# A vision tower on one core: image 0's embedding between position matmuls, one set of norm statistics, stacks per head, images written out

## Chip, cores and metric

One core of one Trainium2 chip runs the kernel. The metric is the device time of one execution in microseconds; the median of the runs counts.

## The reference

Eight images of 3x512x512 become 1024 tokens each of width 256. In float32:

```python
h = patches @ Wp + bp + (relu(xy @ W1 + b1) @ W2 + b2)          # tokens and positions
a = layernorm(h)                                                 # (x - m) / sqrt(var + 1e-5)
n = layernorm(a) * gamma + beta                                  # the attention norms again
q, k, v = split(n @ W_qkv.T); gate = sigmoid(a @ W_gate.T + b_gate)
h = h + a + (attention(q, k, v) * gate) @ W_final.T + b_final    # 8 heads of 32
x = layernorm(h); H = gelu(x @ F1 + c1); p = softmax(H @ Wg + bg)
h = h + p[e] * (H @ Wd[e] + bd[e])                               # e = argmax p, of 8 experts
```

The first norm is taken of h, the second of its result a; both have no weights of their own but gamma and beta.

## The kernel before, in words

Five engines run programs of their own, tied by semaphores. `over_images` (L214) runs `image` for image 0, then three times through a hardware loop whose body is two images (1 to 6), then for image 7. After that come routing (from L1061) and the expert stage over 72 slots of 128 tokens (from L720).

**Opening.** SP loads posin, posw1, posw2 and posbias (L251), 20 constants (L253 to L259), then image 0's tiles into two buffers `xt` (L262). TensorE makes the position table: four K=3 matmuls into banks 0 to 3 (L426), ScalarE's Relu (L758), and for each of eight tiles two matmuls by posw2 (L433) and one K=2 matmul that adds the biases (L434); ScalarE copies to `posb` (L761). Then `front_start` (L604) embeds eight tiles of image 0 (six K chunks each, L444), VectorE adds `posb` (`embedded`, L917), takes statistics of h (`stats`, L899, L903), GpSimd makes rstd (`root`, L339, L342: add eps, then power -0.5), VectorE writes a (L909), does the same on a, and writes n. TensorE transposes n and a (`turn`, L456), projects q and k of the first four heads (`project`, L465), ScalarE and VectorE split them into high and low parts `qk` (L785, L936). fp32 matmuls stand in the trace as two records each.

**Stacks.** `load_stack` (L275) copies, for each of four heads, three high/low pairings of q and of k into `stq` and `stk` (partitions 0 to 31, 32 to 63, 64 to 95), 24 copies of 128 KB, all counted by one semaphore per head group. `score` (L477) waits for all 24 at the group's first step. While they go, TensorE does `values` (L505) and `gates` (L511).

**Steps.** An image has 64 steps, eight token blocks for four heads, twice. Step k: two score matmuls, VectorE's maximum (L1029), ScalarE's Exp (L842), and later `weigh` (L491). Tables (L233 to L244) say at which step TensorE puts in other work: projections of the second group (steps 0 to 7), the next image's embedding (8 to 31), gates, turns and projections of the next image (35 on). At step 32 VectorE does the next image's `norm_1`, `stats_2` and `norm_2` (L1020 to L1026), TensorE the router of the image before (`norm_turn`, `router`), GpSimd both roots, then h + a + b_final (L351, L353) after n is ready. Image 0 has no router in its middle. At an image's start VectorE closes the image before (`gated`, `added` L964, `stats_3`).

## Time and profile before

| | |
|---|---|
| median of 3 runs (1948.21 to 1954.45) | 1952.97 us |
| profiled execution, its own time | 1954.93 us |
| its span | 1952.8 us |
| TensorE, VectorE, ScalarE, GpSimd busy | 89%, 59%, 52%, 16% |
| mean granted TensorE clock | 0.954 |

The span goes from the first to the last instruction; the execution's own time has 2.1 us more. A share of busy time is a mean over stages with different limits.

### The profile page before, as it was taken

The page shows a single profiled execution, that of the slowest core. Times are in us where ns is not written, and L with a number is a line of the kernel's source. Part 1 is how long each engine was busy: PE and PEld are TensorE (multiplying, and loading weights), DVE is VectorE, ACT ScalarE, POOL GpSimd, SP SyncE. Part 2 cuts the span into 40 slices and gives each one's busy share as a digit, 9 for nine tenths or more (in the row PEclk, how much of TensorE's full clock was granted, in tenths as well). Part 3 has the DMA queues.
Part 4 walks back from the last instruction along what each step waited for, and adds up shares of the span by engine and source line. Part 5 has one row for each costly group of instructions (what it writes and reads, how often), then busy time and mean ns, then how long its engine had stood idle before and what let it go on. Part 6 is the DMA issues. An engine that isn't in the chain of part 4 may idle for free.

```text
span 1952.8 us, 32763 instructions
## 1 busy us (share of the span) xinstructions
PE 1728.6 (89%) x11396; PEld 1180.4 (60%) x11396; DVE 1151.3 (59%) x1899; ACT 1012.5 (52%) x1692; POOL 309.7 (16%) x239
## 2 busy tenths in 40 slices
PE   8587899999998999999899999999797724899998
PEld 4354456646655574566467555745363614899998
DVE  0347767467655856675667468566726278344443
ACT  1144756675574657566746656585666350222222
POOL 0200100200010020002000200200000061455554
PEclk9898999999999999999999999999899867899999
DMA  3133042313413140424033222413040160566663
GB/s 112 34 98 98 1 103 77 125 30 99 112 65 82 63 133 28 103 69 133 18 103 92 93 65 73 129 39 87 17 135 1 60 220 1 200 205 199 208 204 132
DMA packets 68112, 187.59 MB, mean 96 GB/s; under 512 B 14173, under 2 KB 14829, under 8 KB 67824
## 3 DMA queue, kind: packets, MB, share of 16 engines
q1 hardware_dynamic: 51952, 121.48, 22.0%
q0 software_dynamic: 16000, 63.98, 10.0%
q8 instruction: 101, 1.65, 0.4%
q14 instruction: 59, 0.48, 0.1%
HBM read 84.72 MB, written 51.38 MB: 70 GB/s over the span
## 4 chain that ended last, share of the span: by engine, by line
PE 72%; DVE 14%; issue 8%; ACT 4%; DMA 1%; SPq 1%; POOL 0%; DVEq 0%; ACTq 0%; POOLq 0%
PE ps L477 12%; PE ps L738 11%; PE ps L491 10%; PE ps L444 8%; DVE nmax L1029 6%; PE ps L548 3%; PE ps L465 3%; PE ps L726 3%; PE ps L549 3%; PE ps L550 3%; PE ps L527 3%; PE ps L505 3%; PE ps L576 3%; ACT pr L842 2%; DVE oh L1084 2%
## 5 line engine op out<-in xcount | busy, mean ns | idle before, releaser
L1029 DVE TENSOR_REDUCE nmax<-ps 128x1 f32<-128x1024 f32 x512 | 625.2, 1222 | 315.1 <-PE ps L477 305.5
L842 ACT ACTIVATE pr<-ps,nmax 128x1024 f32<-128x1024 f32 x512 | 569.9, 1113 | 295.8 <-DVE nmax L1029 290.6
L477 PE MATMUL ps<-stk,stq 96*128 96x512 f32 x1024 | 407.3, 480 | 80.2 <-ACT pr L842 54.1
L477 PEld LDWEIGHTS ps<-stk,stq 96*128 96x128 f32 x1024 | 168.5, 193 | 282.7 <-ACT pr L842 169.0
L491 PE MATMUL ps<-pr,vs 128*32 128x256 f32 x4096 | 275.9, 391 | 16.7 <-DVE vs L948 16.6
L738 PE MATMUL ps<-wd,hg 128*128 x1728 | 225.5, 287 | 0.0
L339 POOL TENSOR_SCALAR vare<-mv 128x8 f32<-128x8 f32 x24 | 5.7, 238 | 1349.8 <-DVE mv L903 1349.8
L738 PEld LDWEIGHTS ps<-wd,hg 128*128 128x128 f32 x1728 | 212.7, 192 | 0.0
L491 PEld LDWEIGHTS ps<-pr,vs 128*32 128x32 f32 x4096 | 109.8, 110 | 166.6 <-issue 75.5
L879 ACT ACTIVATE hg<-ps 128x512 fp32r<-128x512 f32 x144 | 78.5, 596 | 249.6 <-PE ps L726 249.6
L444 PE MATMUL ps<-wp,xt 128*128 128x256 f32 x768 | 198.3, 385 | 1.6 <-DMA xt<-x_in 0.8
L444 PEld LDWEIGHTS ps<-wp,xt 128*128 128x128 f32 x768 | 146.2, 192 | 32.6 <-DMA xt<-x_in 3.1
L811 ACT ACTIVATE ht<-ps,bf 128x512 f32<-128x512 f32 x128 | 88.3, 690 | 115.5 <-PE ps L550 115.5
L465 PE MATMUL ps<-nt,wqk 128*128 128x512 f32 x256 | 132.3, 602 | 3.9 <-DVE qk L936 3.2
L1148 DVE TENSOR_TENSOR hg<-ps,hg 128x512 fp32r<-128x512 f32 x144 | 93.0, 686 | 48.9 <-ACT hg L879 48.8
L548 PE MATMUL ps<-nt_high,wf 128*128 128x512 f32 x256 | 110.7, 432 | 1.7 <-DVE nt_low L985 1.4
L549 PE MATMUL ps<-nt_low,wf 128*128 128x512 f32 x256 | 101.9, 398 | 0.0
L550 PE MATMUL ps<-nt_high,wf 128*128 128x512 f32 x256 | 101.3, 396 | 0.0
L1155 DVE SCALAR_TENSOR_TENSOR rows<-ps,slot_prob,rows 128x256 f32<-128x256 f32 x72 | 34.8, 484 | 111.1 <-PE ps L740 111.1
L842 ACT ACTIVATION_READ_ACCUMULATOR pr<-ps,nmax 128x1 f32 x512 | 99.5, 194 | 0.0
L404 POOL DMA_INDIRECT out<-rows,slot_to x72 | 72.3, 1004 | 123.2 <-DVE rows L1155 116.3
L726 PE MATMUL ps<-ident,rows 128*128 128x128 f32 x576 | 76.4, 277 | 6.6 <-DMA rows<-token_rows,slot_from 6.6
(123 smaller groups left out, 1944.2 us busy)
## 6 DMA issues: line engine op xcount, KB each, us to landing
token_rows<-staged SPq DMA_DIRECT2D x128, 256.0 KB, 2.0
xt<-x_in SPq DMA_DIRECT2D x64, 384.0 KB, 3.1
stq<-qk SPq DMA_DIRECT2D x192, 128.0 KB, 2.4
stk<-qk SPq DMA_DIRECT2D x192, 128.0 KB, 2.5
token_rows<-hres POOLq DMA_DIRECT2D x8, 1024.0 KB, 5.2
wd_raw<-w_down SPq DMA_DIRECT2D x16, 512.0 KB, 4.0
rows<-token_rows,slot_from POOLq DMA_INDIRECT x72, 4.7
out<-rows,slot_to POOLq DMA_INDIRECT x72, 2.6
```

What stands on the lines that cost most here:

```text
L444: last = mm(spare(t)[:, 0:D], xt[:, t % 2, k, :], wp[:, k, :], start=(k == 0), stop=(k == KC - 1))
L465: last = mm(spare(j), wqk[:, c, w * D + g * P:w * D + (g + 1) * P], nt[:, c, hf * HALF:(hf + 1) * HALF], start=(c == 0), stop=(c == DC - 1))
L477: last = mm(ps[:, 2 * (k % SR) + j, :], stq[:, hh, i * P:(i + 1) * P], stk[:, hh, j * 512:(j + 1) * 512], start=True, stop=True)
L491: last = mm(ps[32 * hh:32 * hh + 32, O_BANK + j // 2, (j % 2) * D:(j % 2 + 1) * D], vs[:, gi % 2, hh, :], pr[:, (4 * gi + hh) % PR, j * D: ...
L548: mm(spare(bank), w_high, nt_high[:, c, half], start=(c == 0), stop=False)
L549: mm(spare(bank), w_high, nt_low[:, c, half], start=False, stop=False)
L550: last = mm(spare(bank), w_low, nt_high[:, c, half], start=False, stop=(c == DC - 1))
L726: last = nc.tensor.transpose(ps[:, 2 * (s % 2) + c, q * P:(q + 1) * P], rows[:, s % RING, (4 * c + q) * P:(4 * c + q + 1) * P], ident[:])
L738: mm(o, hg[:, s % 2, h_part, k, :], wd[:, w_part, bass.ds(e, 1), k, :], start=(k == 0 and h_part == w_part), stop=False)
L842: actv(pr[:, k % PR, :], ps[:, 2 * (k % SR):2 * (k % SR) + 2, :].rearrange("p a n -> p (a n)"), ACT.Exp, bias=nmax[:, k % 16:k % 16 + 1], ...
L1029: V.reduce_max(nmax[:, k % 16:k % 16 + 1], ps[:, 2 * (k % SR):2 * (k % SR) + 2, :].rearrange("p a n -> p (a n)"), AX_X, negate=True).then_ ...
L1148: V.tensor_tensor(hg[:, s % 2, 1, 4 * c:4 * c + 4, :].rearrange("p k n -> p (k n)"), ps[:, 2 * (s % 2) + c, :], high_part.bitcast(F32), AL ...
```

## The change

- TensorE does the K=3 matmuls (now in banks 4 to 7), then embeds tiles 0 to 3 of image 0 into banks 0 and 1, then goes on with two position tiles and one embedding tile in turn. Six of image 0's tiles are loaded into free room of `pr`, without waits; ScalarE's queue loads wp, posw2 and posbias (on all partitions). The bias matmul is gone: VectorE adds the bias as it writes `posb`. Seven constants are `early`, twelve are waited for later, and w_ffn1 comes into `hres[:, 1]`.
- a and n are both written from h: rstd of n is (var * (1 + eps) + eps^2)^-0.5; GpSimd makes both with one power on 128x16. n is written first.
- `stq` and `stk` are one tensor; one copy of 256 KB carries a pairing of q and k: 12 a set, each head with its own semaphore, and `score` waits in the first four steps of a group for its head.
- `over_images` writes out all eight images with constant semaphore values.

The diff, without semaphore names and with unchanged lines left out:

```diff
-        stq = tensor(sa, "stq", [96, 4, TOKENS], F32R)
-        stk = tensor(sa, "stk", [96, 4, TOKENS], F32R)
+        st = tensor(sa, "st", [96, 2, 4, TOKENS], F32R)
+        stq, stk = st[:, 0], st[:, 1]
...
-        x_in, stacked = both("x_in"), both("stack")
+        x_in = both("x_in")
+        stacked = [[S[f"stack{g}{hh}"] for hh in range(4)] for g in range(GROUPS)]
+        qk_parts = qk[:].rearrange("p w a t -> p (w a) t")
+        STACK = ((0, 3, 2), (1, 3, 1), (0, 4, 3))
...
-        posbias = at[0:2, 1, 0:D]
-        wf1_in = a[:].rearrange("p (c t) d -> p c (t d)", c=DC)
-        N_CONSTS = 20
+        posbias = at[:, 1, 0:2 * D].rearrange("p (a d) -> p a d", a=2)
+        x_first = pr[:, 2:7].rearrange("p a n -> p (a n)")[:, 0:(TILES - 2) * KC * P].rearrange(
+            "p (t k n) -> p t k n", t=TILES - 2, k=KC)
+        wf1_in = hres[:, 1].rearrange("p (c t) d -> p c (t d)", c=DC)
+        N_CONSTS, N_EARLY = 12, 7
...
-            body(0, 0, False, True)
-            with eng.Fori(0, (IMAGES - 2) // 2) as j:
-                body(j * 2 + 1, 1, True, True)
-                body(j * 2 + 2, 0, True, True)
-            body(IMAGES - 1, (IMAGES - 1) % 2, True, False)
+            for b in range(IMAGES):
+                body(b, b % 2, b > 0, b < IMAGES - 1)
...
-            for dst, src in ((posin, pos_in), (posw1, pos_w1), (posw2, pos_w2), (posbias, pos_bias)):
-                sp.dma_start(dst, src).then_inc(S["pos_in"], 16)
-            for dst, src in ((wp[:], w_patch), (ident[:], identity), (vecs[:, 0, :], ln_gamma),
-                             (vecs[:, 1, :], ln_beta), (vecs[:, 2, :], b_gate), (wqk[:], w_qk), (wv[:], w_v),
-                             (wg[:], w_gate), (wfin[:], w_final), (bfin[:], b_final), (wf1_in, w_ffn1),
-                             (bf1[:], b_ffn1), (wr[:], w_router), (pick[:], pick_in), (up[:], upper),
-                             (rnk[:], rank), (brt[:], b_router), (sst[:], slot_start), (tid[:], token_id),
-                             (col[:], column)):
+            for dst, src in ((posin, pos_in), (posw1, pos_w1)):
+                sp.dma_start(dst, src).then_inc(S["pos_in0"], 16)
+            for t in range(2):
+                sp.dma_start(xt[:, t], x[0, t]).then_inc(x_in[t], 16)
+            for t in range(2, TILES):
+                sp.dma_start(x_first[:, t - 2], x[0, t]).then_inc(S[f"x_first{t // 2 - 1}"], 16)
+            for dst, src in ((vecs[:, 0, :], ln_gamma), (vecs[:, 1, :], ln_beta), (vecs[:, 2, :], b_gate),
+                             (ident[:], identity), (wqk[:], w_qk), (wv[:], w_v), (wg[:], w_gate)):
+                sp.dma_start(dst, src).then_inc(S["early"], 16)
+            for dst, src in ((bfin[:], b_final), (wf1_in, w_ffn1), (wfin[:], w_final), (bf1[:], b_ffn1),
+                             (wr[:], w_router), (pick[:], pick_in), (up[:], upper), (rnk[:], rank), (brt[:], b_router),
+                             (sst[:], slot_start), (tid[:], token_id), (col[:], column)):
...
-                    for r in range(3):
-                        if rear and hh * 3 + r >= 8:
-                            store_hidden(b - 1, hh * 3 + r - 8)
-                        src = slice(32 * hh, 32 * hh + 32)
-                        dst = slice(32 * r, 32 * r + 32)
-                        sp.dma_start(stq[dst, hh, :].bitcast(F32), qk[src, 0, r % 2, :].bitcast(F32)
-                                     ).then_inc(stacked[g], 16)
-                        sp.dma_start(stk[dst, hh, :].bitcast(F32), qk[src, 1, r // 2, :].bitcast(F32)
-                                     ).then_inc(stacked[g], 16)
...
-            load_tile(0, 0)
-            load_tile(0, 1)
-            load_rest(0)
+                    if rear and hh == 3:
+                        for u in range(4):
+                            store_hidden(b - 1, u)
+                    src = slice(32 * hh, 32 * hh + 32)
+                    for r, (first, end, step) in enumerate(STACK):
+                        sp.dma_start(st[32 * r:32 * r + 32, :, hh, :].bitcast(F32),
+                                     qk_parts[src, first:end:step, :].bitcast(F32)).then_inc(stacked[g][hh], 16)
...
-            def root(ln, b):
...
-                hold(pool, f"var{ln}", b + 1)
-                nc.gpsimd.tensor_scalar(vare[:, ln - 1], mv[:, ln - 1, :, 1], EPS, None, ALU.add
-                                        ).then_inc(S[f"eps{ln}"], 1)
-                wait(pool, f"eps{ln}", b + 1)
-                nc.gpsimd.tensor_tensor(rstd[:, ln - 1], vare[:, ln - 1], half_neg[:], ALU.pow
-                                        ).then_inc(S[f"rstd{ln}"], 1)
+            def root_1(b):
...
+                hold(pool, "var1", b + 1)
+                nc.gpsimd.tensor_scalar(vare[:, 0], mv[:, 0, :, 1], EPS, None, ALU.add).then_inc(S["eps1"], 1)
+                nc.gpsimd.tensor_scalar(vare[:, 1], mv[:, 0, :, 1], 1.0 + EPS, EPS * EPS, ALU.mult, ALU.add
+                                        ).then_inc(S["eps1"], 1)
+                wait(pool, "eps1", 2 * b + 2)
+                nc.gpsimd.tensor_tensor(rstd[:, 0:2], vare[:, 0:2], half_neg[:], ALU.pow).then_inc(S["rstd1"], 1)
...
+            def root_3(b):
+                hold(pool, "var3", b + 1)
+                nc.gpsimd.tensor_scalar(vare[:, 2], mv[:, 2, :, 1], EPS, None, ALU.add).then_inc(S["eps3"], 1)
+                wait(pool, "eps3", b + 1)
+                nc.gpsimd.tensor_tensor(rstd[:, 2], vare[:, 2], half_neg[:, 0], ALU.pow).then_inc(S["rstd3"], 1)
...
-                root(1, b)
-                root(2, b)
+                root_1(b)
...
-                hold(pool, "n_ready", b + 1)
+                hold(pool, "a_ready", b + 1)
...
+            pool.wait_ge(S["consts"], 16 * N_CONSTS)
...
-                    root(3, b - 1)
+                    root_3(b - 1)
...
-            root(3, IMAGES - 1)
+            root_3(IMAGES - 1)
...
-            pe.wait_ge(S["pos_in"], 16 * 4)
+            def position(t):
+                o = ps[:, 4 + t // 2, (t % 2) * D:(t % 2 + 1) * D]
+                for c in range(DC):
+                    last = mm(o, posr[:, c, t * P:(t + 1) * P], posw2[:, c, :], start=(c == 0), stop=(c == DC - 1),
+                              skip_group_check=True)
+                last.then_inc(S["pos_mm2"], 1)
...
+            def first_embed(t):
+                if t < 2:
+                    wait(pe, x_in[t], 16)
+                elif t % 2 == 0:
+                    wait(pe, f"x_first{t // 2 - 1}", 32)
+                source = xt[:, t] if t < 2 else x_first[:, t - 2]
+                for k in range(KC):
+                    last = mm(ps[:, t // 2, (t % 2) * D:(t % 2 + 1) * D], source[:, k, :], wp[:, k, :],
+                              start=(k == 0), stop=(k == KC - 1), skip_group_check=True)
+                last.then_inc(S["emb_mm"], 1)
...
+            pe.wait_ge(S["pos_in0"], 16 * 2)
...
-                    mm(ps[:, 2 * c + hf, :], posw1[:, c * P:(c + 1) * P], posin[:, hf * HALF:(hf + 1) * HALF],
+                    mm(ps[:, 4 + 2 * c + hf, :], posw1[:, c * P:(c + 1) * P], posin[:, hf * HALF:(hf + 1) * HALF],
...
+            pe.wait_ge(S["wp_in"], 16)
+            for t in range(4):
+                first_embed(t)
+            pe.wait_ge(S["pos_in1"], 16 * 2)
...
-            pe.wait_ge(S["setup"], 1)
-            for t in range(TILES):
-                o = ps[:, 4 + t // 2, (t % 2) * D:(t % 2 + 1) * D]
-                for c in range(DC):
-                    mm(o, posr[:, c, t * P:(t + 1) * P], posw2[:, c, :], start=(c == 0), stop=False, skip_group_check=True)
-                mm(o, ones[0:2, :].bitcast(F32), posbias, start=False, stop=True, skip_group_check=True).then_inc(S["pos_mm2"], 1)
-            pe.wait_ge(S["pos_done"], 4)
+            for t in range(4):
+                position(2 * t)
+                position(2 * t + 1)
+                first_embed(t + 4)
...
-                    wait(pe, x_in[t % 2], b * 64 + 16 * (t // 2 + 1))
+                    wait(pe, x_in[t % 2], b * 64 - 32 + 16 * (t // 2))
...
-                wait(pe, "n_ready", b + 1)
+                wait(pe, ("n_ready", "a_ready")[w // 2], b + 1)
...
-                if k % G_STEPS == 0:
-                    wait(pe, stacked[g], (b * 24 + 24) * 16)
+                if k % G_STEPS < 4:
+                    wait(pe, stacked[g][hh], (b + 1) * 3 * 16)
...
-                for t in range(TILES):
-                    for part in range(3):
-                        embed(b, t, part)
-                wait(pe, "emb_h", b * TILES + TILES)
+                wait(pe, "pos_done", 4)
...
+            pe.wait_ge(S["early"], 16 * N_EARLY)
+            front_start(0)
...
-            front_start(0)
...
+            nc.scalar.dma_start(wp[:], w_patch).then_inc(S["wp_in"], 16)
+            nc.scalar.dma_start(posw2, pos_w2).then_inc(S["pos_in1"], 16)
+            nc.scalar.dma_start(posbias, pos_bias[None, :, :].broadcast_to([P, 2, D])).then_inc(S["pos_in1"], 16)
...
-                actv(posr[:, j // 2, (j % 2) * HALF:(j % 2 + 1) * HALF], ps[:, j, :], ACT.Relu).then_inc(S["pos_relu"], 1)
-            for j in range(4):
-                act.wait_ge(S["pos_mm2"], 2 * j + 2)
-                actv(posb[:, 2 * j:2 * j + 2, :].rearrange("p t d -> p (t d)"), ps[:, 4 + j, :], ACT.Identity
-                     ).then_inc(S["pos_done"], 1)
...
-            act.wait_ge(S["consts"], 16 * N_CONSTS)
-            actv(wf1[:, 0], wf1_in, ACT.Identity).then_inc(S["wf1_high"], 1)
+                actv(posr[:, j // 2, (j % 2) * HALF:(j % 2 + 1) * HALF], ps[:, 4 + j, :], ACT.Relu).then_inc(S["pos_relu"], 1)
+            act.wait_ge(S["early"], 16 * N_EARLY)
...
-                    if g == 0:
-                        wait(act, stacked[1], b * 24 * 16)
-                    else:
-                        wait(act, stacked[0], (b * 24 + 24) * 16)
+                    for hh in range(4):
+                        if g == 0:
+                            wait(act, stacked[1][hh], b * 3 * 16)
+                        else:
+                            wait(act, stacked[0][hh], (b + 1) * 3 * 16)
...
+            act.wait_ge(S["consts"], 16 * N_CONSTS)
+            actv(wf1[:, 0], wf1_in, ACT.Identity).then_inc(S["wf1_high"], 1)
...
-            dve.wait_ge(S["consts"], 16 * N_CONSTS)
+            dve.wait_ge(S["pos_in1"], 16 * 2)
+            V.tensor_tensor(posbias[:, 0], posbias[:, 0], posbias[:, 1], ALU.add).then_inc(S["pos_sum"], 1)
+            dve.wait_ge(S["early"], 16 * N_EARLY)
...
-            dve.wait_ge(S["setup"], 2)
-            dve.wait_ge(S["wf1_high"], 1)
-            V.tensor_tensor(wf1[:, 1], wf1_in, wf1[:, 0].bitcast(F32), ALU.subtract
-                            ).then_inc(S["setup"], 1)
...
+                aggregate(b, ln)
...
+            def aggregate(b, ln):
...
-                hold(dve, f"rstd{ln}", b + 1)
+                hold(dve, "rstd1", b + 1)
...
-                    last = V.tensor_scalar(dst[:, t, :], src[:, t, :], mv[:, ln - 1, t, 0:1],
-                                           rstd[:, ln - 1, t:t + 1], ALU.subtract, ALU.mult)
+                    last = V.tensor_scalar(dst[:, t, :], src[:, t, :], mv[:, 0, t, 0:1], rstd[:, ln - 1, t:t + 1],
+                                           ALU.subtract, ALU.mult)
...
-                wait(dve, "emb_mm", b * TILES + t + 1)
+                wait(dve, "emb_mm", b * TILES + (t + 1 if b else t // 2 * 2 + 2))
...
-                V.tensor_tensor(hres[:, par, t, :], spare(t)[:, 0:D], posb[:, t, :], ALU.add).then_inc(S["emb_h"], 1)
+                source = spare(t)[:, 0:D] if b else ps[:, t // 2, (t % 2) * D:(t % 2 + 1) * D]
+                V.tensor_tensor(hres[:, par, t, :], source, posb[:, t, :], ALU.add).then_inc(S["emb_h"], 1)
...
-                normalise(a, hres[:, par], b, 1, "a_ready")
...
-            def stats_2(b):
-                wait(dve, "a_ready", b + 1)
-                stats(a, b, 2)
...
-            def norm_2(b, before):
...
+            def norm_2(b, par, before):
...
-                normalise(n, a, b, 2, "n_ready")
+                normalise(n, hres[:, par], b, 2, "n_ready")
+                normalise(a, hres[:, par], b, 1, "a_ready")
...
+            dve.wait_ge(S["pos_sum"], 1)
+            dve.wait_ge(S["setup"], 2)
...
+                if t % 2 == 0:
+                    wait(dve, "pos_mm2", t + 2)
+                    V.tensor_tensor(posb[:, t:t + 2, :], ps[:, 4 + t // 2, :].rearrange("p (t d) -> p t d", t=2),
+                                    posbias[:, 0, None, :].broadcast_to([P, 2, D]), ALU.add).then_inc(S["pos_done"], 1)
+                    wait(dve, "pos_done", t // 2 + 1)
...
-            norm_1(0, 0)
-            stats_2(0)
-            norm_2(0, False)
+                if t >= 1:
+                    wait(dve, "emb_h", t)
+                    V.bn_stats(bst[:, 0, t - 1, :], hres[:, 0, t - 1, :])
+            wait(dve, "emb_h", TILES)
+            V.bn_stats(bst[:, 0, TILES - 1, :], hres[:, 0, TILES - 1, :]).then_inc(S["stats1"], 1)
+            aggregate(0, 1)
+            norm_2(0, 0, False)
...
+            dve.wait_ge(S["wf1_high"], 1)
+            V.tensor_tensor(wf1[:, 1], wf1_in, wf1[:, 0].bitcast(F32), ALU.subtract).then_inc(S["setup"], 1)
...
-                            stats_2(b + 1)
...
-                            norm_2(b + 1, before)
+                            norm_2(b + 1, 1 - par, before)
```

## Rows read from the trace of the kernel before

**Rows 1.** The page's fourth part: the chain that ended last, by engine.

```profile
PE 72%; DVE 14%; issue 8%; ACT 4%; DMA 1%; SPq 1%; POOL 0%; DVEq 0%; ACTq 0%; POOLq 0%
```

**Rows 2.** Windows, one image each: length, engines busy, PEclk, DMA share, GB/s.

```profile
254.97:432.31 177.34, 168.92 (x1106) 105.84 (x1105) 117.45 (x201) 113.25 (x192) 16.03 (x9) 1.00 0.30 84
...
609.58:793.72 184.14, 173.19 (x1106) 108.51 (x1105) 117.55 (x201) 113.36 (x192) 15.86 (x9) 0.97 0.29 81
793.72:972.22 178.50, 170.08 (x1105) 106.00 (x1104) 117.59 (x201) 113.98 (x193) 15.86 (x9) 0.99 0.30 84
972.22:1155.59 183.37, 173.03 (x1106) 108.47 (x1105) 117.24 (x200) 112.64 (x190) 15.86 (x9) 0.97 0.29 81
1155.59:1332.90 177.31, 168.90 (x1105) 105.82 (x1105) 117.35 (x201) 113.27 (x192) 15.86 (x9) 1.00 0.30 84
```

**Rows 3.** Chain of waits of the opening: start us, us, what.

```profile
4.40 7.21 PE ps L426 x8
...
12.28 2.07 PE ps L433 x4
14.35 1.15 PE ps L434 x2
...
38.26 5.50 PE ps L444 x12
...
61.69 2.87 PE ps L444 x12
```

**Rows 4.** Timeline, opening, norms: start, us, engine, line, operation.

```profile
64.58 0.42 DVE L917 TENSOR_TENSOR hres<-ps,posb 128x256 f32<-128x256 f32 x1 [2.52 <-PE ps L444]
...
67.79 0.64 DVE L903 BATCH_NORM_AGGREGATE mv<-bst 128x2 f32<-128x6 f32 x8
68.62 0.24 POOL L339 TENSOR_SCALAR vare<-mv 128x8 f32<-128x8 f32 x1 [67.63 <-DVE mv L903]
68.95 1.67 POOL L342 TENSOR_TENSOR rstd<-vare,half_neg 128x8 f32<-128x8 f32 x1
...
81.70 1.94 PE L456 MATMUL ps<-ident,n 128*128 128x128 f32 x8 [17.16 <-DVE n L909]
```

**Rows 5.** Timeline, opening, stacks and first scores.

```profile
97.81 0.61 SPq L285 DMA_DIRECT2D stq<-qk  x1
...
115.81 1.22 PE L477 MATMUL ps<-stk,stq 96*128 96x512 f32 x2 [7.37 <-DMA stk<-qk]
...
122.15 0.73 PE L477 MATMUL ps<-stk,stq 96*128 96x512 f32 x2 [0.34 <-ACT pr L842]
```

**Rows 6.** Timeline, middle of image 0, VectorE.

```profile
179.61 2.70 DVE L899 BATCH_NORM_STATS2 bst<-hres 128x6 f32<-128x256 f32 x8
...
197.09 2.36 DVE L1029 TENSOR_REDUCE nmax<-ps 128x1 f32<-128x1024 f32 x2
```

**Rows 7.** Timeline, start of image 1: first copy, fourth score.

```profile
254.05 0.53 SPq L285 DMA_DIRECT2D stq<-qk  x1
...
278.83 0.90 PE L477 MATMUL ps<-stk,stq 96*128 96x512 f32 x2
```

**Rows 8.** Waits: VectorE for the router's partial logits.

```profile
DVE lt L992 <- PE ps L558: 77.1, 16, 17.6
```

**Rows 9.** Windows of the opening: as in rows 2.

```profile
4.40:12.20 7.80, 7.19 (x8) 2.49 (x8) 0.00 (x0) 2.36 (x4) 0.00 (x0) 1.00 1.02 369
...
108.50:115.80 7.30, 0.00 (x0) 0.00 (x0) 0.00 (x0) 0.66 (x1) 0.00 (x0) 0.79 0.91 195
```

**Rows 10.** The page's sixth part: one group of copies, us to landing.

```profile
stq<-qk SPq DMA_DIRECT2D x192, 128.0 KB, 2.4
```

**Rows 11.** Chain of waits, start of image 1 and first return of the loop.

```profile
254.97 3.65 PE ps L505 x16
...
609.58 2.69 issue
612.27 6.47 PE ps L505 x16
```

8 lines of the change are left out of this document (4 added, 4 removed).

## The prediction

> **What bounds the kernel now.** I read the chain of waits first. TensorE carries 72% of it and VectorE 14% [rows 1]; no transfer bounds the whole, so a part of the change counts only where TensorE stands still or works on something avoidable. The table by image comes next: the six images between the first and the last take 177.3 us three times, and 184.1, 178.5 and 183.4 us the other times [rows 2]. The last two-thirds of the span are thus a steady machine, with irregularities at two places. The opening is the opposite: the first score matmul of image 0 starts at 115.8 us, and before it the chain is a list of single engines, one after another [rows 3 to 5]. After that I looked at the middle of image 0, the only one that has no router of an earlier image between its two head groups [rows 6], at the start of image 1 [rows 7], and at who waits during the routers [rows 8].
>
> **Opening, tokens (front part).** Now: first matmuls at 4.40, when the last of four small loads has landed; 7.21 us for the K=3 matmuls; eight position tiles of 2.01 + 1.15 us, to 37.6; the first embedding tile 5.50 us, the later ones 2.87 us, with a 0.3 us wait for the input buffer between them, the last ending at 64.56 [rows 3]. After: only two small loads stand before the first matmul; issued 0.7 us earlier, so it starts at 3.7 and the K=3 matmuls end at 10.9. wp now comes on ScalarE's queue behind at most a table load of 1.28 us, and shares the engines with the eight image tiles. wp and the first four tiles are 2.3 MB; at the 369 GB/s of the opening [rows 9] that is 6.3 us, landed by about 10, and tiles 2 and 3 are wanted only near 19. All other early constants are 2 MB more and wanted at 50. I therefore cost the loads at nothing; were they not covered, SP's issue (0.4 us a load) would delay wp's neighbours by 2 to 3 us.
>
> What remains is TensorE's rate. The profile's granted clock is 1.00 from the start [rows 9], but the same 128x256 matmuls take half a microsecond per record until 43.8 us and a quarter afterwards [rows 3]: I go by durations, so this is the lower level (1.2 GHz), then the higher (2.4 GHz). It rose 5.5 us after TensorE had gone over to nothing but full K=128 matmuls, and not in 26 us of busy position work with K=2 matmuls among it. Image 0 goes over to full matmuls at 10.9, so one tile at 5.5 and three at 2.87 end at 25.0. Then four rounds of two position tiles (2 x 4 records of 0.24 us = 1.9; the bias matmuls, 1.15 us each, are gone, VectorE adds the bias) and one embedding tile (2.87): 19.1 us, to 44.1. VectorE's work of a round is one 128x512 addition (at most two of 0.42 [rows 4]), two of 0.42 and two statistics of 0.34 (an eighth of 2.70 [rows 6]), 2.4 us beside TensorE's 4.8: hidden. Gain here: 64.6 - 44.1 = **20.4 us**.
>
> The rule of the Trainium skill that bears on this, "TensorE: Matmul & The Clock Gate", section "What's actually happening", says that the throttled state is the default and that busy time releases it. By it the clock would be up before the embedding starts, and the sum 2.6 us lower. The trace does not agree: busy throughout and slow for 39 us.
>
> **Opening, norms.** Now 0.42 us for the last addition, 2.7 + 0.64 for the statistics, POOL's root, 2.7 for a, then all of it again for n: TensorE transposes at 81.70, 17.1 us after the embedding [rows 4]. After: five of the eight statistics run beside TensorE; two additions, three statistics, the aggregation and gaps leave 2.7 us instead of 3.9. POOL then does two cheap operations (0.24) and one pow on 128x16. The trace has pow only at 128x8: 1.67 us [rows 4]. Bounds: 1.67 (all fixed) and 3.34 (all per element). A cheap operation of the same size takes 0.24, so little is fixed: 3.2 us. Root with gaps 4.0, n 2.7, start 0.1: the transposes begin 9.5 us after the embedding. The transposes of a wait until 2.7 us after n, where now they follow the 1.94 us of n's [rows 4] at 2.05: 0.7 lost. Gain: 17.1 - 9.5 - 0.7 = **6.9 us**. POOL's two additions of 4.5 us start after a is ready and are wanted only at the end of image 0.
>
> wf1's two halves move behind the projections of image 0; ScalarE (1.9 us) and VectorE (2.3 us) are otherwise idle while TensorE does values and gates (10.7 us). Nothing.
>
> **Opening, stacks.** Now 24 copies are issued 0.64 us apart from 97.81 and the first score waits for all: 18.0 us [rows 5], although TensorE had finished values and gates after 10.7 (7.37 us wait [rows 5]). The fourth score starts 24.3 us after the first issue. The DMA engines are 0.91 busy at 195 GB/s in that stretch [rows 9], so 12 copies of twice the size can't go much faster: I take 15.5 us for the set plus 2.1 to land, 17.6 for head 3; heads 0, 1, 2 at about 6, 10, 14. The scores of heads 0 to 2 then start at 10.7, 12.4 and 14.8, and the fourth at 17.6, where head 3 binds. Gain at the fourth: **6.7 us**. Bounds: 0 and 7.4.
>
> **Middle of image 0.** VectorE's chain from 179.61 to the maximum at 197.09 [rows 6] loses one set of statistics (3.4 us) and one root (2.1), and gains 1.5 + 0.3 for the wider root: **3.7 us**. The stack for the second group is late next, but only its first heads are wanted at once: head 0 at 183, head 3 near 194, its score near 197.5. That the scores wait for stk meanwhile is a wait beside VectorE's, and doesn't count twice.
>
> **Images 1 to 7.** The saved statistics save nothing: VectorE stands still for the router's partial logits 77 us in all [rows 8]. n and a now follow each other behind keep_logits, 2.7 us more there, more than 10 us before its next maximum. At an image's start the stack is issued from 254.05, its last copy lands 18 us later, near 272, and TensorE comes to the fourth score at 278.83 [rows 7]: hidden before and after. In the second group the router covers both; the four hidden stores now stand together ahead of head 3, and end in the router too.
>
> **Images written out.** The loop comes back twice. At 609.58 TensorE issues nothing for 2.69 us, and its next matmuls take 6.47 us, where the same ones take 3.65 us in image 1 [rows 11]: 5.5 us of image 3's surplus of 6.8 over 177.3 [rows 2]. That leaves 1.3 us for some matmuls at the lower level later in the image; image 4, which no return precedes, has a surplus of 1.2 too, and image 5's 6.1 are then a return of 4.8 and 1.3. The granted clock of these three is 0.97, 0.99 and 0.97, of the others 1.00 [rows 2]. Entering and leaving the loop costs nothing visible. I take the 10.3 us of the two returns and, as the short falls came in half the images, about a third of the other 3.8: **11.5 us**. Bounds: 0 (nothing bound to the loop) and 14.1.
>
> **Sum:** 20.4 + 6.9 + 6.7 + 3.7 + 11.5 = 49.2 us. The profiled execution took 1954.9 us: 1905.7; it is 2.0 us above the median of the three runs (1952.97), so the median becomes 1903.8, **1904 us**. Image 7's end, routing and the expert stage (from 1521 us) are not touched.
>
> **Rivals.**
> - *The clock stays low.* If position work among the embedding keeps TensorE at the lower level, eight tiles of 5.5 and eight of 2.01 end at 10.9 + 60.1 = 71.0, not 44.1: 27 us dearer, **1931 us**. For: the slow 26 us of position work [rows 3]. Against: K=2 matmuls are gone, and four full tiles stand ahead. 0.09.
> - *The clock rises with any busy time*, so already in the K=3 matmuls, and the first embedding tile takes 2.87 in place of 5.50: 2.6 us less, **1901 us**. Against: 39 slow us. 0.04. This is the rule of the Trainium skill named above.
> - *Returns cost the same without a loop*, as stretches of fetching code that the loop only happens to show: no 11.5 us, **1915 us**. This is also the case in which writing out doesn't do what it should. Against: image 6, reached in straight code, has no surplus, and image 1, the first inside, has none either [rows 2]. 0.10.
> - *Slower: the paired copies.* Each copy now gathers two strided rows of qk per partition. If the set of 12 takes S us instead of 18, the fourth score of every later image is late by S - 24.8 (254.05 to 278.83 [rows 7]), seven times; image 0 loses S - 17.6 at its start and about S - 21 in its middle. It eats the 49 us at S = 29, that is 2.4 us a copy where two now take 1.28. At twice the present time, S = 36: 78 + 18 + 15 = 111 us, **2015 us**. For: no such pattern in the trace. Against: of the 2.4 us to a 128 KB copy's landing [rows 10] the bytes at 195 GB/s are 0.7, the rest has nothing to do with size, and the pieces per partition stay 4 KB long. 0.04.
> - My forecast: 0.73.
>
> **Range.** Own bounds of the likeliest: down by 2.6 (clock), 3 (pow, twice), 0.7 (stacks) and 2.6 (loop), 9 us: 1895; up by two more slow tiles (5.3), loads (2.5), stacks (3), loop (5) and VectorE's round (1): 1921. That takes in two rivals; 1931 and 2015 stay out, so 1895 to 1922. What a measurement can tell from no change is 0.3%, 6 us; every case but the last is far beyond it: faster 0.94, same 0.02, slower 0.04.
>
> **What would show it.** First score of image 0 near 82 us in place of 115.8; embedding of image 0 ended near 44 with 2.87 us tiles from the second on; one pow of about 3.2 us per image; six middle images at 177 to 179 us; no issue gap at 610 and 972. Wrong, if embedding tiles stay at 5.5 us, if TensorE waits for stacks at image starts, or if the middle images keep 180 us and more.

## Result and profile after

| | before | after |
|---|---|---|
| median of four runs | 1953.31 us (1948.21 to 1954.45) | 1896.16 us (1895.51 to 1899.28) |
| span of the profiled execution | 1952.8 us | 1896.9 us |
| mean granted TensorE clock | 0.954 | 0.964 |

The kernel is faster: ratio 0.9715, 95% interval 0.9695 to 0.9736. The forecast was 1904 us with a range of 1895 to 1922; the gain is 57.2 us by the medians and 55.9 us by the spans, against a sum of 49.2. The working below goes by the spans of one profiled execution each (that of after is the slowest of its four), which are cut at four instants: end of the opening (fourth score matmul of image 0), first values matmul of image 1, the same of image 7, end.

| stretch | before | after | gain | forecast |
|---|---|---|---|---|
| start to fourth score | 122.15 | 86.11 | 36.0 | 34.0 |
| to image 1 | 132.8 | 129.8 | 3.0 | 3.7 |
| images 1 to 6 | 1077.9 | 1062.3 | 15.6 | 11.5 |
| image 7 to the end | 619.9 | 618.7 | 1.3 | 0 |

The chain by engine, fourth part of the page after; it answers to [rows 1]:

```profile
PE 72%; DVE 13%; issue 7%; ACT 5%; DMA 2%; SPq 1%; POOL 0%; DVEq 0%; ACTq 0%; POOLq 0%
```

"DMA" rose from 1% to 2%: transfers bind in a few places more, the opening above all. Its chain shows them (start us, us, what; it answers to [rows 3 to 5]):

```profile
1.22 4.24 DMA pr<-pos_w
5.50 7.19 PE ps L449 x8
12.69 12.05 PE ps L442 x48
24.74 1.73 PE ps L431 x8
26.46 2.59 PE ps L442 x12
...
39.41 2.60 PE ps L442 x12
...
45.35 2.95 POOL rstd L342
48.32 2.67 DVE n L932 x8
...
59.56 7.15 PE ps L489 x16
...
80.93 5.14 DMA st<-qk
86.11 0.73 PE ps L501 x2
```

Read it as a ladder. The second of two small loads lands late, and TensorE starts at 5.50, 1.1 us later than before. The first four embedding tiles take 12.05 us; four at the later pace (2.59) would take 10.4, so little of this stretch was slow. Then rounds of 1.73 and 2.59 follow without a gap, to 42.0 us (before 64.56). One power, then n (a and the transposes follow in lines left out); the projections start at 59.56. The last step is a transfer: the copy for head 3 lands 5.1 us after its issue, and the fourth score waits for it.

The middle of image 0, VectorE's timeline (as [rows 6]):

```profile
144.53 2.70 DVE L919 BATCH_NORM_STATS2 bst<-hres 128x6 f32<-128x256 f32 x8
...
151.57 2.67 DVE L932 TENSOR_SCALAR n<-hres,mv,rstd 128x256 f32<-128x256 f32 x8 [3.66 <-POOL rstd L342]
...
157.93 2.34 DVE L1061 TENSOR_REDUCE nmax<-ps 128x1 f32<-128x1024 f32 x2
```

From statistics to maximum 13.4 us, before 17.5 [rows 6]: 4.1 gained. One us of that is not a loss of this stretch: a pair of projections at half speed (1.71 us instead of 0.86) stood before the fourth score in the kernel before and stands behind it now, at 89.14.

The windows by image (columns as in [rows 2]):

```profile
215.92:392.47 176.55, 168.82 (x1105) 105.71 (x1105) 113.83 (x185) 113.23 (x192) 15.55 (x8) 1.00 0.31 84
...
922.08:1101.68 179.60, 170.31 (x1105) 105.91 (x1105) 113.85 (x185) 113.30 (x192) 15.39 (x8) 0.99 0.30 83
1101.68:1278.21 176.53, 168.78 (x1106) 105.65 (x1105) 113.85 (x185) 113.20 (x192) 15.39 (x8) 1.00 0.31 84
```

Five of the six images take 176.5 us, three of which had 177.3 [rows 2]: 0.8 us that no step of the forecast contained. VectorE is 3.5 us less busy in each, the saved statistics; that is not where the 0.8 are from (experiments 1 and 5). The waits say where those went: VectorE now waits 129.8 us for the router's partial logits, before 77.1 [rows 8].

```profile
DVE lt L1012 <- PE ps L582: 129.8, 16, 17.4
```

ScalarE's timeline has the 0.8 us. Image 1 before:

```profile
374.08 0.60 ACT L798 ACTIVATE staged<-ps 128x512 f32<-128x512 f32 x1 [0.40 <-DMA token_rows<-staged]
375.34 1.28 ACT L842 ACT_TABLE_LOAD   x1 [0.66 <-DVE nmax L1029]
```

And after:

```profile
334.63 0.60 ACT L818 ACTIVATE staged<-ps 128x512 f32<-128x512 f32 x1 [0.24 <-DMA token_rows<-staged]
335.24 1.28 ACT L864 ACT_TABLE_LOAD   x1
```

The Exp needs a table that the router's Gelu displaced. Before, the load of 1.28 us itself waited for the maximum; after, it starts with the end of the last `staged` copy. In the groups of instructions, the seven loads of before (images 1 to 7) stand in one row, with 4.0 us of idle time ahead of them; in after it is 0.1:

```profile
L842 ACT ACT_TABLE_LOAD x7 | 9.0, 1283 | 4.0 <-DVE nmax L1029 4.0
```

Image 5 of after is 3.1 us longer. The chain has one transfer there at nearly twice its usual time, the twelfth of the sixteen stores of the router's hidden values (`staged`) in that image. It takes 2.0 us as a rule, and ScalarE waits for its buffer:

```profile
1038.76 3.42 DMA token_rows<-staged
```

### The profile page after: what moved, and what is told of

It is laid out like the page before. It is cut to its first block, busy times and chain, and to the rows that moved or that the text cites. A ratio compares the mean times of both kernels' runs of the same rounds, so it can differ in the third digit from the quotient of the medians.

```text
span 1896.9 us, 29956 instructions
## 1 busy us (share of the span) xinstructions
PE 1696.9 (89%) x11380; PEld 1165.0 (61%) x11380; DVE 1125.5 (59%) x1776; ACT 1009.6 (53%) x1688; POOL 306.0 (16%) x231
## 3 DMA queue, kind: packets, MB, share of 16 engines
q0 software_dynamic: 16000, 63.98, 10.4%
## 4 chain that ended last, share of the span: by engine, by line
PE 72%; DVE 13%; issue 7%; ACT 5%; DMA 2%; SPq 1%; POOL 0%; DVEq 0%; ACTq 0%; POOLq 0%
PE ps L501 12%; PE ps L760 11%; PE ps L515 11%; PE ps L468 8%; DVE nmax L1061 5%; PE ps L572 3%; PE ps L748 3%; PE ps L489 3%; PE ps L574 3%; PE ps L573 3%; ACT pr L864 3%; PE ps L551 3%; PE ps L529 3%; PE ps L600 2%; DVE oh L1116 2%
## 5 line engine op out<-in xcount | busy, mean ns | idle before, releaser
L501 PE MATMUL ps<-st 96*128 96x512 f32 x1024 | 403.8, 477 | 69.3 <-ACT pr L864 54.6
L501 PEld LDWEIGHTS ps<-st 96*128 96x128 f32 x1024 | 167.0, 192 | 272.3 <-ACT pr L864 140.9
L468 PE MATMUL ps<-wp,xt 128*128 128x256 f32 x672 | 172.8, 378 | 0.0
L468 PEld LDWEIGHTS ps<-wp,xt 128*128 128x128 f32 x672 | 126.3, 189 | 25.3 <-DVE qk L956 1.3
L346 POOL TENSOR_SCALAR vare<-mv 128x8 f32<-128x8 f32 x8 | 1.9, 239 | 718.5 <-DVE mv L926 718.5
L1012 DVE COPY lt<-ps 128x512 f32<-128x512 f32 x16 | 11.1, 692 | 129.8 <-PE ps L582 129.8
```

The source lines that it names most:

```text
L468: last = mm(spare(t)[:, 0:D], xt[:, t % 2, k, :], wp[:, k, :], start=(k == 0), stop=(k == KC - 1))
L501: last = mm(ps[:, 2 * (k % SR) + j, :], stq[:, hh, i * P:(i + 1) * P], stk[:, hh, j * 512:(j + 1) * 512], start=True, stop=True)
```

## Experiments

Every kernel was measured beside the kernel before on the same chip; those medians are 1951.3 to 1952.6 us.

**1. The loop alone, written out** in the kernel before:

```diff
-            body(0, 0, False, True)
-            with eng.Fori(0, (IMAGES - 2) // 2) as j:
-                body(j * 2 + 1, 1, True, True)
-                body(j * 2 + 2, 0, True, True)
-            body(IMAGES - 1, (IMAGES - 1) % 2, True, False)
+            for b in range(IMAGES):
+                body(b, b % 2, b > 0, b < IMAGES - 1)
```

> The kernel before, its image loop written out, nothing else. Then the six middle images take 176.5 us each (177.3, 184.1, 178.5, 183.4 before), 15 to 19 us in all, and the time is about 1936. Rival: the 0.8 us per image belongs to the stacks or the norms; then the images stay at 177.3, the gain is 14 us or less and the time 1939 or more. Second rival: it is fetching that the loop only shows; no gain, 1953.

Measured: 1937.28 us, ratio 0.9917 (0.9889 to 0.9946), 15 us less. Windows of images 1, 2 and 5:

```profile
254.15:436.43 182.28, 172.94 (x1105) 108.41 (x1105) 117.39 (x201) 113.20 (x192) 16.03 (x9) 0.97 0.29 82
436.43:613.00 176.57, 168.80 (x1105) 105.69 (x1105) 117.34 (x201) 113.23 (x192) 15.89 (x9) 1.00 0.30 84
...
966.49:1147.37 180.88, 171.60 (x1105) 106.53 (x1105) 117.24 (x201) 113.22 (x192) 15.86 (x9) 0.98 0.29 82
```

The base of 176.5 us is there with the old norms and old copies, and the table load's idle time is 0.1 us. So the 0.8 us per image belong to the loop. Laid side by side, TensorE's matmuls in image 1 of the kernel before stay within 0.3 us of those in image 2 of this one up to the table load, and are 0.6 to 1.1 us late from there on.

Images 1 and 5 are longer than the base by 10.1 us together: the twelfth hidden store takes 3.92 and 3.84 us there, and the granted clock falls to 0.97 and 0.98. So the six images gain only 8.2 us in this execution (1069.8 against 1077.9); 4.6 us more of its span's gain lie behind image 7's start, where nothing was changed, and are spread.

**2. Without the K=2 matmuls.** The kernel before, with no bias added to the position table:

```diff
-                    mm(o, posr[...], posw2[:, c, :], start=(c == 0), stop=False, ...)
-                mm(o, ones[0:2, :].bitcast(F32), posbias, start=False, stop=True, ...).then_inc(S["pos_mm2"], 1)
+                    last = mm(o, posr[...], posw2[:, c, :], start=(c == 0), stop=(c == DC - 1), ...)
+                last.then_inc(S["pos_mm2"], 1)
```

> The kernel before without the K=2 matmul that adds the biases to a position tile (the biases are left out of the result). Theory: the K=2 matmuls keep TensorE at the lower level; without them it rises some 4 us into the position tiles, their last records take 0.22 us in place of 0.50, position ends near 22 us in place of 37.6 and the first embedding tile takes 2.6 us in place of 5.5: 18 us less, 1935. Rival: only the embedding raises the rate; records stay at 0.50, position ends near 28.4, the first embedding tile still takes 5.5: 9 us less, 1944.

Measured: 1934.26 us (one run). Its chain:

```profile
12.39 9.24 PE ps L433 x32
...
22.31 2.87 PE ps L445 x12
```

The 32 position records take 9.24 us; in the kernel before they take 16 (eight times 2.01), with 9.2 of bias matmuls between them [rows 3]. The first embedding tile is fast at once.

**3. K=2 replaced by K=128.** The same work for TensorE, at full height, with another bias in the sums:

```diff
-                mm(o, ones[0:2, :].bitcast(F32), posbias, start=False, stop=True, ...)
+                mm(o, ones[:].bitcast(F32), posw2[:, 0, :], start=False, stop=True, ...)
```

> The kernel before with the K=2 bias matmul replaced by one with K=128 (ones by the first chunk of posw2 in place of the biases, so the biases in the result are others): the same number of matmuls, columns and weight loads. Theory: few rows of the array at work keep the clock low; with 128 rows it rises some 4 us into the position tiles, which end near 25 us in place of 37.6, and the first embedding tile is fast: 15 us less, 1938. Rival: the number of short matmuls and the pauses between groups keep it low, however many rows: no change, 1953.

Measured: 1942.18 us (one run). Its chain:

```profile
15.16 1.71 PE ps L433 x4
16.87 0.85 PE ps L434 x2
17.72 1.03 PE ps L433 x4
18.75 0.43 PE ps L434 x2
```

The pairs halve at 17.7 us (0.85 to 0.43, and the groups of four from 1.71 over 1.03 to 0.86), though the instructions are as many as before. What kept TensorE slow for 39 us was thus the low matmuls and what comes with them, not the number of matmuls. One thing changed together with the height: at the same lower level four records and a pair take 1.71 and 0.85 us here, where the kernel before needs 2.01 and 1.15, 0.3 us more at every change between K=128 and K=2. This experiment doesn't show that these pauses had no part in it. The K=3 matmuls have no such changes among them, though, and 7.2 us of them left the level low too. Image 1 starts 13.5 us earlier (241.49); images 1 to 6 took 1079.8 us in this execution, 1.9 more than in the kernel before.

**4. A semaphore per head, 24 copies as before:**

```diff
-                if k % G_STEPS == 0:
-                    wait(pe, stacked[g], (b * 24 + 24) * 16)
+                if k % G_STEPS < 4:
+                    wait(pe, stacked[g][hh], (b + 1) * 6 * 16)
```

> The kernel before with one semaphore per head for the same 24 copies of 128 KB. Theory: the gain of the stacks comes from the semaphores alone, since the engines set the pace of the set: first score of image 0 10.7 us after the first issue in place of 18.0, the fourth about 18 in place of 24.3; 5 to 6 us less, 1947.5. Rival: pairing q and k is needed; with 24 copies head 3 lands after 20 us or more and the gain is under 3 us. In images 1 to 7 nothing in either.

Measured: 1946.06 us, ratio 0.9971 (0.9957 to 0.9984). The first copy is issued at 97.04; the scores of heads 0 and 1 start at 107.1 and 108.4, those of heads 2 and 3, from the timeline:

```profile
111.35 0.73 PE L478 MATMUL ps<-stk,stq 96*128 96x512 f32 x2 [1.03 <-DMA stk<-qk]
...
115.35 0.74 PE L478 MATMUL ps<-stk,stq 96*128 96x512 f32 x2 [2.41 <-DMA stk<-qk]
```

The fourth comes 18.3 us after the first issue, against 24.3 before and 18.0 after (68.08 to 86.11). Nearly all of the stack term is the finer wait; pairing q and k in one copy neither helps nor hurts by more than 0.3 us.

**5. The shared statistics alone** in the kernel before (n and a both from h, one power on 128x16):

```diff
-                normalise(n, a, b, 2, "n_ready")
+                normalise(n, hres[:, par], b, 2, "n_ready")
+                normalise(a, hres[:, par], b, 1, "a_ready")
```

> The kernel before with the changed kernel's norms alone (one set of statistics, one power on 128x16, n and a both from h, n first). Theory: a gain only in image 0, where nothing covers the chain: 4.9 us in the opening (one set of statistics 3.4, one root 2.1, less 1.3 for the wider power and 0.2 for its second cheap operation, and 0.6 back because a comes last), 4.1 us in its middle, nothing in images 1 to 7, where VectorE goes on waiting for partial logits: 8 to 9 us in all, 1944. Rival: images 1 to 6 gain 0.8 us each too, since VectorE is free earlier; then 1939, and images of 176.5 us inside the loop.

Measured: 1944.08 us, ratio 0.9959 (0.9943 to 0.9974). Timeline of its opening, and the first score of the middle:

```profile
68.76 2.94 POOL L343 TENSOR_TENSOR rstd<-vare,half_neg 128x16 f32<-128x16 f32 x1
...
74.56 1.94 PE L461 MATMUL ps<-ident,n 128*128 128x128 f32 x8 [10.48 <-DVE n L914]
...
188.33 2.08 PE L482 MATMUL ps<-stk,stq 96*128 96x512 f32 x4 [12.36 <-DMA stk<-qk]
```

The power takes 2.94 us. The first score comes 5.8 us earlier (110.0 against 115.8), image 1 starts 7.8 earlier (247.17), so the middle gives 2.0. There VectorE's chain has shrunk, but the one semaphore for 24 copies now ends last and returns the rest. In images 1 to 6 nothing is won: image 1 takes 177.3 us, as before. This is the check on the saved statistics: 3.4 us less work an image, no time.

**6. Position tiles first, then the embedding,** in the kernel after:

```diff
-            for t in range(4):
-                first_embed(t)
-            pe.wait_ge(S["pos_in1"], 16 * 2)
-            pe.wait_ge(S["pos_relu"], 4)
-            for t in range(4):
-                position(2 * t)
-                position(2 * t + 1)
-                first_embed(t + 4)
+            for t in range(TILES):
+                position(t)
+            pe.wait_ge(S["wp_in"], 16)
+            for t in range(TILES):
+                first_embed(t)
```

> The changed kernel with its eight position tiles ahead of its eight embedding tiles, not between them. Theory: the order is worth next to nothing; what it replaced was slow for its K=2 matmuls and for the waits for the input. TensorE waits 0.7 us for the last Relu, the position tiles take the slow start instead of the embedding, and VectorE's additions, which now come in one row at the end, still keep up with 2.6 us a tile: image 0's embedding ends 0 to 1.5 us later, 1896 to 1898. Rival: the position tiles between the embedding hide VectorE's and the loads' work; without them the first transposes come 4 us later or more, 1900.

Measured: 1892.71 us, ratio 0.9691 (0.9674 to 0.9707), no slower than after; the forecast was 1896 to 1898. Its chain:

```profile
13.23 9.12 PE ps L431 x32
22.35 20.73 PE ps L442 x96
```

The embedding ends at 43.1 instead of 42.0, and image 1 starts at 217.23 instead of 215.92. Neither is beyond chance: in after and in kernels 9, 11 and 12, whose openings are the same code, the embedding ends at 42.0, 43.4, 42.1 and 43.0, the fourth score starts at 86.1 to 87.3, and image 1 at 215.9 to 218.5. The order that gives the change its name is worth nothing that can be told; the token term is the missing bias matmuls, the clock that rises early without them, and the loads that no longer wait for a buffer.

**7. Image 1's norms spread over image 0's steps** (statistics beside the embedding from step 8 on, two of the 16 writes of n and a in each of the steps 34 to 41):

```diff
+                    if after and not before and G_STEPS + 2 <= k < G_STEPS + 10:
...
+                        for t in (m % 4 * 2, m % 4 * 2 + 1):
+                            last = V.tensor_scalar(dst[:, t, :], hres[:, 1 - par, t, :], mv[:, 0, t, 0:1],
+                                                   rstd[:, ln - 1, t:t + 1], ALU.subtract, ALU.mult)
```

> The changed kernel with image 1's norms spread over image 0's steps (statistics tile by tile behind the embedding in steps 8 to 31, the power beside gated and two maxima, n and a two tiles a step in steps 34 to 41), images 2 to 7 as they are. Theory: in the middle of image 0 two chains run side by side, VectorE's (13.4 us from 144.5) and the copies of the second group's heads (18 us from 141.7, head 3 at 159.8). With VectorE's gone the copies bind, and the fourth score of the group, now at 161.7, comes near 159.8: only 1 to 2 us less, 1894. Rival: VectorE's chain is what sets it and the copies have room; then 9 us less, 1887.

**8. The same, with each head's copies released by that head's last score:**

```diff
-                hold(sp, "score_mm", b * STEPS + g * G_STEPS)
                 for hh in range(4):
+                    hold(sp, "score_mm", b * STEPS + g * G_STEPS - 3 + hh)
```

> The kernel a_mid with, besides, each head's copies released by that head's own last score (steps 28 to 31) in place of the last score of all heads. Theory: the set of copies starts 5.5 us earlier, head 3 lands near 154, and both chains are gone together: the fourth score of the second group near 154 in place of 161.7; 7 to 8 us less than the changed kernel, 1888. In images 1 to 7 the copies are hidden before and after. Rival: the earlier copies take the engines from the input loads or the stores of other images and cost in all eight images; then 1896 or more.

Measured: 1892.68 us (one run) for 7 and 1894.25 us, ratio 0.9702 (0.9686 to 0.9718), for 8. Timeline of the second head group's last score that waits, in 7 and then in 8:

```profile
159.60 1.22 PE L501 MATMUL ps<-st 96*128 96x512 f32 x2 [2.35 <-DMA st<-qk]
```

```profile
155.74 1.22 PE L501 MATMUL ps<-st 96*128 96x512 f32 x2 [2.22 <-DMA st<-qk]
```

With VectorE's norms out of the way the copies bind, as forecast (159.8), and releasing them earlier moves the score up by 3.9 us (forecast 154). But image 1 starts at 217.93 in 7 and at 214.93 in 8, against 215.9 to 218.5 for after's opening: of the 6 us by which kernel 8 beats after's 161.7 at that score, 1 to 3.6 are left, and the 1888 us forecast for it are missed. The norms had been moved into steps that VectorE's maximum already paces, so they came back one step at a time. The chain of 8 shows the pattern:

```profile
164.25 1.23 DVE nmax L1065
165.47 0.64 DVE a L1090 x2
166.12 1.13 DVE nmax L1065
```

**9. Idle matmuls as filler** in the last image's steps, to keep the clock up where the kernel after shows 0.95 for the image:

```diff
+                    if not after and (11 <= k < G_STEPS or k >= G_STEPS + 8):
...
+                        mm(spare(k)[:, 0:D], xt[:, 0, 0, :], wp[:, 0, :], start=True, stop=True)
```

> The changed kernel with one idle matmul (two records of 0.22 us, result unused) a step in steps 11 to 31 and 40 to 63 of the last image, which has no embedding, turns or projections of a next one. Theory: the last image takes 181 to 188 us from run to run because TensorE has pauses there and its granted clock falls (1.00 in the run with 181.4, 0.83 and 0.95 in two stretches of the changed kernel's with 187.5); VectorE and ScalarE set the pace at 1.69 us a step, so the idle matmuls fit into the pauses, keep the clock at 1.00, and the last image takes 181 to 182: 1891 to 1892. Rival: the fillers lengthen the steps (they stand in TensorE's queue before the next scores), 46 times 0.1 us or more, and give back what the clock saves: 1896 or more, the last image at 186.

**10. Everything together:** the fillers, the earlier copies, image 1's statistics and norms in two halves (steps 23 to 31 and 34 to 37), and the big loads held back until the two small ones are in:

```diff
+            sp.wait_ge(S["pos_in0"], 32)
             for t in range(2):
                 sp.dma_start(xt[:, t], x[0, t]).then_inc(x_in[t], 16)
...
+            act.wait_ge(S["pos_in0"], 32)
             nc.scalar.dma_start(wp[:], w_patch).then_inc(S["wp_in"], 16)
```

> The changed kernel with four things: the fillers of a_warm; each head's copies released by its own last score; image 1's norms in two halves, of which the first (four tiles) is done in image 0's steps 10 to 31, where TensorE sets the pace, and the second after step 32; wp and the image tiles issued only once the two loads of the first matmuls have landed. Theory: fillers 5 us, middle of image 0 about 4 (image 1 starts near 211 in place of 215.9; a_both showed that operations moved to steps 34 to 41 are only moved, so only the first half is hidden), first matmul at 4.0 in place of 5.5: 10 us less than the changed kernel, 1886. Rival: the small operations among the steps cost what they save, as in a_both; then only the fillers and the loads are left, 1890.

**11. The kernel after with the loop put back** (the reverse of experiment 1):

> The changed kernel with the image loop back in place, everything else as changed. Theory: the loop costs the same here as in the kernel before, where writing it out alone gave 15 us: two returns of 5 to 6 us with the slow matmuls after them, and 0.7 us an image for the table load behind a wait on a register (its loads start 0.6 to 0.7 us late again): 1896 + 15 = 1911. Rival: the gains overlap, since per-head semaphores also make the images of the loop faster; then 1906 or less.

**12. The kernel after once more,** unchanged, beside 9 to 11:

> The changed kernel again, beside the three others on their chip, as what they are compared with: 1896, its last image between 181 and 188 us by chance of the clock.

| | median, us | ratio to before | span | image 7 to the end |
|---|---|---|---|---|
| 9 fillers | 1895.94 (1891.04 to 1902.17) | 0.9719 (0.9696 to 0.9742) | 1893.0 | 615.3 |
| 10 all | 1889.73 (1887.39 to 1892.99) | 0.9685 (0.9668 to 0.9703) | 1887.9 | 617.4 |
| 11 loop | 1914.57 (1912.49 to 1927.21) | 0.9833 (0.9800 to 0.9865) | 1910.7 | 615.8 |
| 12 after | 1898.03 (1895.23 to 1903.65) | 0.9722 (0.9703 to 0.9741) | 1901.4 | 614.3 |

The fillers gain nothing that can be told: the last stretch takes 614.3 us without (12) and 615.3 or 617.4 with them. The forecast of 1891 to 1892 us for 9 is missed, and its rival, longer steps, fits better: image 7 from its first values matmul to its last `weigh` takes 176.6 us in 9 and 179.4 in 10, against 175.1 in 12 and 172.2 in 7, both without fillers. Nor do fillers decide the clock. In 10, with fillers:

```profile
1392.00:1453.00 61.00, 55.60 (x385) 30.40 (x385) 40.71 (x49) 37.20 (x62) 0.00 (x0) 0.94 0.00 1
```

and in 7, without:

```profile
1399.00:1460.00 61.00, 44.73 (x348) 21.65 (x346) 41.56 (x53) 35.23 (x60) 0.00 (x0) 1.00 0.00 1
```

TensorE is busier in the first and was granted less; in 9, also with fillers, the same part is granted 1.00 at 54.44 us busy of 60. What decides the clock there stays open.

Kernel 10 has the lowest median, 8.3 us below its neighbour 12 (the intervals of their ratios touch at 0.9703; its slowest run is 2.2 us faster than the fastest of 12). Its forecast of 1886 us is missed by 3.7; the rival stood at 1890. Its chain begins

```profile
1.22 1.44 DMA pr<-pos_w
2.70 7.19 PE ps L464 x8
```

The same small load takes 1.44 us from issue to landing instead of 4.24, and TensorE starts 2.8 us earlier; the large loads, delayed, still arrive in time. Image 1 starts at 211.55, 4.4 us before the kernel after and 6.5 before 12. Of the 4.4, 2.2 exist at the fourth score already (83.87), the other 2.1 are the middle. The rest of its lead is that ScalarE never waited for a late store in images 1 to 6 (1059.0 us in all, against 1062.3 in after and 1069.0 in 12). Kernel 9, whose images 1 to 6 are after's code, has 1059.1, so this part is chance and not one of its four changes.

Putting the loop back costs 16.5 us against 12 (forecast 15). The chain at its first return:

```profile
571.09 2.98 issue
574.07 6.10 PE ps L532 x16
```

This is the pair of lines from [rows 11] again: a gap, then values matmuls of 6.10 us that take 3.65 elsewhere. The Trainium skill says in "Runtime: NRT & Kernel Launch", section "Instruction fetch mechanics", that a taken branch out of the current pages makes the engine fetch code before it can go on. The gaps of 2.98 and 2.86 us at the two returns, and none in the written-out kernels, agree with it.

## Why the prediction was right, step by step

**Where the gain would come from: right.** All the places are where they were put; three of the five terms came within 0.7 us. The total is less good than that: 1896.16 us lies 1.2 us above the lower end of the range, 7.8 below the forecast. Of the signs named in advance, the first score came at 78.2 us (near 82 forecast), the embedding ended at 42.0 (near 44), and five middle images took 176.5 (177 to 179).

**Tokens, 20.4 forecast, 22.5 measured** (64.56 to 42.02). Three sizes were off, in both directions:
- First matmul at 5.50, not 3.7. The step "I therefore cost the loads at nothing" failed. It counted bytes until a tile was wanted, and forgot that the two small loads stand in the same DMA engines as eight tiles and wp issued right behind them. Experiment 10 shows the price, 2.8 us. That the term came within 2.1 us all the same is partly luck: matmuls started 1.8 us late and then took 3.9 us less than set.
- Four first tiles in 12.05 us, not 14.1, and tiles at 2.59, not 2.87. The 2.87 of [rows 3] is a tile that starts behind a wait; back to back it costs 0.28 less. Four such tiles at full speed make 10.4, so the slow part cost 1.7, where 2.6 were set.
- Two position tiles 1.73, not 1.92, by the same argument.

**The clock: mechanism right.** That it rises behind full-height matmuls and not in position work with K=2 among it was read from one row; experiments 2 and 3 show it from both sides. The rival by which any busy time raises it needed a fast first embedding tile behind the slow K=3 matmuls; these took 7.19 us again, the embedding's first records were slow too, and kernel 3, with K=128 in place of K=2, got its clock at 17.7 us.

**Norms, 6.9 forecast, 7.2 measured** (end of the embedding to the first projection: 24.7 to 17.5 us). The power on 128x16 was taken as 3.2 between bounds of 1.67 and 3.34; it is 2.94.

**Stacks, 6.7 forecast, 6.3 measured** (projections to fourth score: 32.9 to 26.6). The set lands at 18.0, forecast 17.6. Experiment 4 shows that the cause is the wait per head. The slower rival, paired copies, is excluded: 12 of 256 KB take what 24 of 128 KB take.

**Middle, 3.7 forecast, 4.1 measured on VectorE's chain,** 3.0 at image 1, since a slow pair of projections crossed the border. That the saved statistics would save nothing later is confirmed by experiment 5.

**Images written out, 11.5 forecast, 15.6 measured.** This is the mis-sized term. Two things were wrong in it. First, "entering and leaving the loop costs nothing visible" looked for a cost at the borders and took the 177.3 us of an image as the base. Every image inside paid 0.8 us more, 4.6 us in six, since ScalarE's table load stood behind the wait for the maximum (0.66 us idle ahead of it). The row of waits said it (4.0 us in six instances, ScalarE at the Exp, which is one per loop image) and was passed over as small. Second, the step took a third of the surplus other than the returns; all of it went. Against a base of 176.53 the six images before have 18.7 us too much, of which after returns all but the 3.1 of one late store. Putting the loop back gives the same account from the other side: 177.3, 177.8, 183.9, 177.8, 184.3 and 177.8 us, 19.7 above the base. The rival by which returns cost the same without a loop falls with experiment 1.

**Last stretch, nothing forecast, 1.3 measured.** The same code took 613.3 to 619.9 us in the profiled executions, so this is spread, not effect. The other executions of after's opening (experiment 6) have the fourth score up to 1.2 us later and image 1 up to 2.6, so the terms before image 1 aren't known to tenths either.

The errors of the terms are +2.1, +0.3, -0.4, -0.7, +4.1 and +1.3, together 6.7: the sum was low mainly because one cost of the loop was missed. The error of that term would be 7.2, had no store been late in the profiled execution of after.

## What to carry to other kernels

Before pricing a loop's removal, compare an image inside the loop with the same code outside it, instruction by instruction and not only at the borders: here a table load sat behind a wait in the one and ahead of it in the other. A small load that starts the critical path should have the DMA engines to itself; holding the large ones back until it has landed was worth 2.8 us and needed two waits. Moving work off an engine's chain pays only if the steps that receive it are not paced by the same engine, and if what ends last next (here the copies) moves too.

## What the runs showed of the hardware

- With 16 K=2 records among 32 full ones TensorE stayed at the lower level (1.2 GHz by the durations) to 44.4 us; with K=128 in their place the higher (2.4 GHz) came at 17.7, and without them near 17. In after it came 3 us into the full matmuls, behind 7.2 us of K=3 matmuls at the lower level. The clock column shows 1.00 in all these stretches, so durations are the safer witness there.
- A change between K=128 and K=2 matmuls cost 0.3 us at the lower level (2.01 and 1.15 us for four records and two, against 1.71 and 0.85 with one height).
- A ScalarE table load is placed behind a wait in the loop and ahead of the wait in written-out code (0.66 us idle in each of six images, against 0.1 in all seven). The loop's waits compare with a value in a register, the written-out ones with a constant. That this is what decides is inferred; the runs changed both together.
- Copies within the on-chip memory move as fast in 12 pieces of 256 KB (18.0 us to the last head's score) as in 24 of 128 KB (18.3 us).
- In every profiled kernel some hidden stores take more than 2.7 us, up to 4.6, in place of about 2 (16 of 128 in after, 20 in before). In the images 1 to 6 of the written-out kernels this cost time only where the twelfth store of an image was among them, for whose buffer ScalarE waits: 3.42 us in image 5 of after, 3.74 and 3.10 in images 1 and 5 of its repetition, 3.92 and 3.84 in experiment 1. It costs 3 to 7 us an image, as the clock can fall behind it. In kernel 10 the three stores behind the twelfth are late instead (4.18, 4.04 and 3.81 us in image 1), and nothing waits for them.
- During each of these late stores a packet of 16 KB goes through an instruction queue. In after it begins at 1039.44 us and takes 1.23 us, inside the late store issued at 1038.76. Packets of 8 or 16 KB on the instruction queues overlap 14 of after's 16 slow stores and 9 of the other 112, but in before only 10 of 20, against 15 of 108. That the packet delays the store is likely from this and not shown: no experiment moved it. The DMA view of after from 1038 to 1042.5 us has

```profile
q8 instruction: 1, 0.02, 1.7%
```
